# A convolution pair on one core: the residual added by the storing DMA, and TensorE's pieces dealt out anew

## The reference

```
x1  = x  + blur4x4(gn(x))                      # layer 0, gn: 32 groups
out = x1 + sum over 9 taps of wgt[tap] * shifted(gn(x1))   # layer 1
wgt = w2 . relu(group_norm(d4_1x1(gn(x1), w1))) + b2
```

## Time and profile before

| | |
|---|---|
| time, median of 3 runs | 5196.06 us (5190.89 to 5196.19) |
| the profiled execution's own time | 5190.41 us |
| its span | 5188.6 us |
| first stage | to about 1150 us |
| busy: PE, DVE, ACT, POOL | 4650.8, 4464.1, 2864.1, 3903.4 us |
| DMA | 679.71 MB, 131 GB/s on average |

### The profile page before, as it was taken

How to read it: one execution, slowest core, us unless ns; L and a number is a source line. 1 busy time by engine, 2 the same in 40 slices (tenths; PEclk the granted TensorE clock), 3 DMA queues, 4 the chain that set the end, 5 groups by cost and what they waited for, 6 DMA issues and landing times.

```text
span 5188.6 us, 117277 instructions
## 1 busy us (share of the span) xinstructions
PE 4650.8 (90%) x39036; PEld 1648.4 (32%) x39036; DVE 4464.1 (86%) x7761; ACT 2864.1 (55%) x4642; POOL 3903.4 (75%) x1952
## 2 busy tenths in 40 slices
PE   8999999978989898988989898989898989898965
PEld 3333333322333232333333232323232323232322
DVE  6777777734989898989899999989898989898998
ACT  7999999955444444444445454444444444444421
POOL 6888888833878787777777787778787868787888
PEclk9999999989999999999999999999999999999987
DMA  8999999943333233333333233333332323332321
GB/s 237 257 257 257 257 256 256 247 107 90 102 102 115 87 113 97 106 99 103 99 103 109 93 111 99 106 95 115 99 111 91 115 91 111 99 116 90 105 71 65
DMA packets 872972, 679.71 MB, mean 131 GB/s; under 512 B 560224, under 2 KB 822752, under 8 KB 856032
## 3 DMA queue, kind: packets, MB, share of 16 engines
q1 hardware_dynamic: 872416, 672.79, 44.2%
HBM read 404.21 MB, written 268.44 MB: 130 GB/s over the span
## 4 chain that ended last, share of the span: by engine, by line
PE 40%; DVE 16%; issue 12%; POOL 7%; ACT 3%; DVEq 0%; POOLq 0%; DMA 0%; SPq 0%; ACTq 0%
PE ps L801 8%; PE ps L748 7%; POOL acc L1054 7%; PE ps L803 6%; PE ps L738 6%; PE ps L789 5%; DVE prod_d L1105 5%; PE ps L776 5%; DVE prod_p L1105 4%; DVE ps L1149 3%; PE ps L763 2%; DVE ps L1105 2%; DVE six_t L1070 1%; DVE acc L1151 1%; ACT xh L901 1%
## 5 line engine op out<-in xcount | busy, mean ns | idle before, releaser
L1054 POOL TENSOR_TENSOR acc<-acc,prod_p 128x1024 f32<-128x1024 f32 x1280 | 3040.7, 2376 | 848.1 <-DVE acc L1151 701.0
L1105 DVE TENSOR_TENSOR prod_p<-ps,val 128x1024 f32<-128x1024 f32 x1280 | 1555.0, 1215 | 39.8 <-issue 27.8
L1105 DVE TENSOR_TENSOR prod_d<-ps,val 128x512 f32<-128x512 f32 x1536 | 1042.6, 680 | 10.7 <-ACT ps L959 10.7
L299 PE MATMUL ps<-xn,band 64*64 64x512 f32 x8192 | 948.0, 598 | 21.4 <-issue 12.9
L801 PE MATMUL ps<-acc,base 128*128 128x512 f32 x1024 | 620.6, 690 | 335.3 <-DVE prod_d L1105 311.2
L748 PE MATMUL ps<-xh,wh 128*32 128x512 f32 x6144 | 729.1, 602 | 70.5 <-ACT xm L909 24.8
L331 POOL TENSOR_TENSOR x_out<-x_out,x_in 128x512 f32<-128x512 f32 x512 | 636.4, 1275 | 0.0
L259 ACT ACTIVATE x_out<-ps 64x512 f32<-64x512 f32 x1024 | 606.2, 592 | 50.4 <-PE ps L299 28.7
L959 ACT ACTIVATE ps<-ps,b 128x256 f32<-128x256 f32 x576 | 236.7, 445 | 664.7 <-PE ps L789 661.4
L803 PE MATMUL ps<-prod_d,base 128*128 128x512 f32 x1024 | 589.4, 661 | 0.0
L776 PE MATMUL ps<-xm,base 128*32 128x256 f32 (+1 forms) x8192 | 574.8, 418 | 2.5 <-ACT xm L933 2.4
(11 more groups left out here) (76 smaller groups left out, 3706.8 us busy)
## 6 DMA issues: line engine op xcount, KB each, us to landing
x_in<-x SPq DMA_DIRECT2D x128, 1024.0 KB, 7.4
x<-x_out SPq DMA_DIRECT2D x256, 512.0 KB, 5.2
xr<-x SPq DMA_DIRECT2D x512, 256.0 KB, 3.4
acc<-x SPq DMA_DIRECT2D x1024, 128.0 KB, 3.1
out<-acc SPq DMA_DIRECT2D x256, 512.0 KB, 2.7
prod_p<-wsrc SPq DMA_DIRECT2D x1, 384.0 KB, 5.3
w<-w2t SPq DMA_DIRECT2D x1, 288.0 KB, 5.1
shift_m<-shifts SPq DMA_DIRECT2D x1, 256.0 KB, 5.7
```

Source lines behind the costliest of these rows:

```text
L299: mm = nc.tensor.matmul(ps[to:to + H2, 2 * two + t, :], band[rows, v, rows], group(xn[rows, k % N_RING, :], XP, W, v, 2 * two + x), start= ...
L1054: nc.gpsimd.tensor_tensor(acc[:, r, :], acc[:, r, :], prod_p[:, k % P_RING, :], ALU.add).then_inc(p_added, 1)
L1105: return nc.vector.tensor_tensor(dst.rearrange("p (m r w) -> p m r w", m=count, w=W), taps_of(tap).rearrange("p (m r w) -> p m r w", m=1, ...
```

## The change

The residual no longer goes through `acc` and TensorE. SyncE copies x1, in the output's layout, from DRAM to DRAM into `out` (two granules ahead as before); GpSimd, after the five adds of a granule, issues the storing DMA itself, with `accum_op=add`, so that the store adds `acc` onto the copy. For this GpSimd waits for its own last add and for the copy (`resid_in`). TensorE adds one product instead of two. VectorE waits for the store of four granules earlier before it writes `acc`. Values are made two granules ahead instead of three, the pieces stand in other half-steps, and the third block of statistics moves from granule 11 to 13.

```diff
-AHEAD = GRANS - 1
+AHEAD = GRANS - 2
-FORWARD_1 = {3: ((2, 1),), 5: ((3, 0),), 7: ((4, 1),), 9: ((5, 0),)}
-FORWARD_2 = {0: ((0, 0), (0, 1)), 1: ((1, 0), (1, 1)), 2: ((2, 0),), 5: ((3, 1),), 6: ((4, 0),), 9: ((5, 1),),
-             10: ((6, 0), (6, 1)), 12: ((7, 0), (7, 1))}
-BLOCK_V_1 = {1: ((0, 0), (0, 1)), 2: ((1, 0),), 6: ((3, 0), (3, 1)), 10: ((5, 0), (5, 1)), 14: ((7, 0), (7, 1))}
-BLOCK_V_2 = {2: ((1, 1),), 4: ((2, 0), (2, 1)), 8: ((4, 0), (4, 1)), 13: ((6, 0), (6, 1))}
-BLOCK_T_1 = {5: (2,), 9: (4,), 13: (7,)}
-BLOCK_T_2 = {1: (0,), 2: (1,), 6: (3,), 10: (5,), 12: (6,)}
-INVERSE_1 = {2: (0,), 3: (1,), 7: (3,), 11: (5,), 13: (6, 7)}
-INVERSE_2 = {5: (2,), 9: (4,)}
-LOAD_AT = {1: 1, 2: 2, 4: 3, 6: 4, 8: 5, 10: 6, 11: 7}
-LOAD_NEXT_AT = 13
+FORWARD_1 = {3: ((2, 1),), 5: ((3, 1),), 7: ((4, 1),), 10: ((6, 0), (6, 1)), 11: ((7, 0), (7, 1))}
+FORWARD_2 = {0: ((0, 0), (0, 1)), 1: ((1, 0), (1, 1)), 2: ((2, 0),), 4: ((3, 0),), 6: ((4, 0),),
+             8: ((5, 0), (5, 1))}
+BLOCK_V_1 = {1: ((0, 0),), 14: ((7, 0), (7, 1))}
+BLOCK_V_2 = {2: ((0, 1),), 4: ((1, 0), (1, 1)), 5: ((2, 0), (2, 1)), 6: ((3, 0), (3, 1)), 9: ((4, 0), (4, 1)),
+             10: ((5, 0), (5, 1)), 13: ((6, 0), (6, 1))}
+BLOCK_T_1 = {1: (0,), 2: (1,), 5: (2,), 6: (3,), 9: (5,), 12: (7,)}
+BLOCK_T_2 = {8: (4,), 10: (6,)}
+INVERSE_1 = {2: (0,), 7: (3,), 13: (7,)}
+INVERSE_2 = {2: (1,), 5: (2,), 9: (4,), 12: (5, 6)}
+LOAD_AT = {1: 1, 2: 2, 4: 3, 6: 4, 8: 5, 9: 6, 10: 7}
+LOAD_NEXT_AT = 12
...
-                dst = acc[32 * q:32 * q + 32, r, :].rearrange("p (m n) -> p m n", m=QM)
+                dst = out[img, at, 32 * q:32 * q + 32].rearrange("p (m n) -> p m n", m=QM)
                 sp.dma_start(dst, src).then_inc(resid_in[r], 16)
-        def store(i, n):                     # SyncE
-            wait_apart(sp, sp_apart, p_added, i * (NP * N_GRAN) + NP * (n + 1))
...
-            sp.dma_start(out[img, m], acc[:, n % ACC_RING, :]).then_inc(stored[n % ACC_RING], 16)
...
-            if half == 0:                    # add_two, now add_one
-                pe.wait_ge(resid_in[n % ACC_RING], i * (64 * N_GRAN // ACC_RING) + 64 * (n // ACC_RING + 1))
-            nc.tensor.matmul(ps[:, D_BANK, :], same, acc[:, n % ACC_RING, half * HALF:(half + 1) * HALF],
-                             start=False, stop=False, skip_group_check=True)
...
+        def store(i, n):                     # GpSimd, called after the five adds of granule n
+            r = n % ACC_RING
+            pool.wait_ge(p_added, i * (NP * N_GRAN) + NP * (n + 1))
+            pool.wait_ge(resid_in[r], i * (64 * N_GRAN // ACC_RING) + 64 * (n // ACC_RING + 1))
+            nc.gpsimd.dma_start(out[i, n], acc[:, r, :], accum_op=ALU.add).then_inc(stored[r], 16)
...
+            if a == 0 and not first(i, n - ACC_RING + 1):      # VectorE, before L1151
+                dve.wait_ge(stored[r], i * (16 * N_GRAN // ACC_RING) + 16 * (n // ACC_RING))
...
-            if more and n == 11:
+            if more and n == 13:
                 t_stats(i + 1, 2)
-            if more and n == 13:
                 t_stats(i + 1, 3)
```

More of the change, by code:

```diff
@@ L653, in load_x, with copy_resid @@
                 sp.dma_start(xr[:, kt, :].rearrange("p (q n) -> p q n", q=2), src).then_inc(x_loaded, 16)
-        def load_resid(i, n):
+        def copy_resid(i, n):
             u, q4, r = (n // GRANS) % UNITS, n % GRANS, n % ACC_RING
@@ L659, in load_resid @@
                 wait_apart(sp, sp_apart, stored[r], i * (16 * N_GRAN // ACC_RING) + 16 * (n // ACC_RING))
-            img = i + n // N_GRAN
+            img, at = i + n // N_GRAN, n % N_GRAN
             for q in range(BANDS):
@@ L663, in load_resid @@
                     :, q4 * QM:(q4 + 1) * QM, (q * 16 + u * UR) * W:(q * 16 + (u + 1) * UR) * W]
-                dst = acc[32 * q:32 * q + 32, r, :].rearrange("p (m n) -> p m n", m=QM)
+                dst = out[img, at, 32 * q:32 * q + 32].rearrange("p (m n) -> p m n", m=QM)
                 sp.dma_start(dst, src).then_inc(resid_in[r], 16)
-        def store(i, n):
-            wait_apart(sp, sp_apart, p_added, i * (NP * N_GRAN) + NP * (n + 1))
-            img, m = (i + n // N_GRAN, n % N_GRAN) if n >= 0 else (i - 1, n + N_GRAN)
-            sp.dma_start(out[img, m], acc[:, n % ACC_RING, :]).then_inc(stored[n % ACC_RING], 16)
         sp.dma_start(base[:], basis[:, 0:4 * P]).then_inc(base_in, 16)
@@ L681, in _, with period @@
             load_x(0, c)
-        load_resid(0, 0)
-        load_resid(0, 1)
+        copy_resid(0, 0)
+        copy_resid(0, 1)
         load_x(1, 0)
-        def period(i, more=True, ahead=True, begin=False):
+        def period(i, more=True, ahead=True):
             for n in range(N_GRAN):
@@ L692, in period @@
                 if more or n + 2 < N_GRAN:
[L693 to L697, removed]
+                    copy_resid(i, n + 2)
+        period(0)
         with sp.Fori(1, B - 2) as i:
@@ L701, in _ @@
         period(B - 1, more=False, ahead=False)
-        store(B - 1, N_GRAN - 1)
         for r in range(ACC_RING):
+            sp.wait_ge(resid_in[r], 64 * B * N_GRAN // ACC_RING)
             sp.wait_ge(stored[r], 16 * B * N_GRAN // ACC_RING)
@@ L794, in tap_weights, with add_one @@
                 mm.then_inc(tap_mm, 1)
-        def add_two(i, n, half):
+        def add_one(i, n, half):
             pe.wait_ge(own, i * (OWN * N_GRAN) + OWN * n + OWN // 2 * half + 2)
-            if half == 0:
-                pe.wait_ge(resid_in[n % ACC_RING], i * (64 * N_GRAN // ACC_RING) + 64 * (n // ACC_RING + 1))
-            nc.tensor.matmul(ps[:, D_BANK, :], same, acc[:, n % ACC_RING, half * HALF:(half + 1) * HALF],
-                             start=False, stop=False, skip_group_check=True)
             nc.tensor.matmul(ps[:, D_BANK, :], same, prod_d[:, 0, :], start=False, stop=True, skip_group_check=True)\
@@ L835, in _ @@
         values(1)
-        values(2)
         def half_step(i, n, of_t, of_inverse, of_v, of_forward):
@@ L851, in period @@
                 u = n // GRANS
-                add_two(i, n, 0)
+                add_one(i, n, 0)
                 if n % GRANS == 0 and not (begin and n == 0):
@@ L862, in period @@
                         values(1)
-                        values(2)
-                add_two(i, n, 1)
+                add_one(i, n, 1)
                 if more:
@@ L987, in _ @@
         keep_values(0, 1)
-        keep_values(0, 2)
         def keep_half_step(i, n, of_t, of_inverse, of_v, of_forward):
@@ L1015, in period @@
                         keep_values(i + 1, 1)
-                        keep_values(i + 1, 2)
                         relu(i + 1, 0)
@@ L1056, in period @@
                         t_rstd_of(i + 1)
+                store(i, n)
         period(0)
```

## The result

The changed kernel takes 5064.98 us (median of 4 runs, 5061.32 to 5067.52) against 5193.48 for the kernel before beside it (5189.98 to 5196.19): a ratio of 0.9752, 95% interval 0.9736 to 0.9769. The forecast was 5088. The profiled span is 5065.8 us, 122.8 shorter than before. In the new file L1142 is the old L1149, L1146 the old L1151, L1098 makes the products, L793 is TensorE's add, L1046 GpSimd's adds, L1035 its DMA, L666 the copies.

The account below looks back on a forecast made before the run. VectorE and TensorE, both near 91% busy, took turns as the bound. -16.4 + 3.5 + 4.6 + 1.2 = -7.1 us an image, -106 over 15, then -4 and +2: 5082 profiled, 5088 median; range 4990 to 5250.

Parts of the forecast that it names:

- TensorE off VectorE's path: Second stage: without the residual's matmul, VectorE's wait for TensorE falls from 16.4 to 3.5 us an image, gaining 12.9.
- GpSimd the new bound, by a little: GpSimd's adds plus a 1.2 us store take 13.65 us a granule against VectorE's 13.23: 4.6 us an image.
- The last image: Its granules, 13.9 us each before, would take 13.65 (-4 us); the last store, issued later, adds 2.
- my own formula: Change an image for an issue of d us: -16.4 + 3.5 + d + 11 (d - 0.78); gain gone at 1.79.
- The 13.23: Time in us that VectorE needs for a granule in which it does not wait.
- the ring: Four product buffers between VectorE and GpSimd: last pooled product begins 10.2 us after VectorE's last sum, needing four adds, 10.0.
- the slack can't be saved up: With only four product buffers, GpSimd's store costs 0.42 us in each of 11 granules without extra VectorE work.
- The image's change: Where images turn, the store of granule 13 stands between GpSimd's power and granule 14: cost 1.2 us.
- The hidden issue: Rival: GpSimd's store issue takes 0.78 us or less and VectorE is the bound: 5010 us; chance 0.17.
- Slower by the issue: Rival: GpSimd's issue makes it the bound in earnest: 5284 us at 2.2, 5382 at 2.7; chance 0.18.
- A product of VectorE in flight: Rival: GpSimd's issue waits for VectorE's running product, up to 1.2 us more, 2.4 in all: 5324 us; chance 0.04.
- Half clock: Rival: TensorE, less busy, is granted a mean clock of 0.8 and holds VectorE again: 5190 us; chance 0.11.

Follow-up runs that it names:

- tap1_twice: The changed kernel with tap 1's product added twice by TensorE, one matmul more in each half: 5187.84 us, ratio 0.9990 to the kernel before.
- dma_old_order: The changed kernel with the old order of TensorE's pieces, values three granules ahead and third statistics after granule 11: 5056.58 us, ratio 0.9736 to the kernel before.
- sync_plain: The changed kernel with SyncE storing acc plainly, the residual left out of the output and no DMA on GpSimd: 4960.70 us, ratio 0.9551 to the kernel before.
- store_behind: The changed kernel with GpSimd's store of granule n-1 issued after the fifth add of granule n: 5009.09 us, ratio 0.9644 to the kernel before.
- two_issues: The changed kernel with each GpSimd store split into two DMAs of 64 partitions, same bytes: 5212.36 us, ratio 1.0038 to the kernel before.

## Why the prediction was right, point by point

**TensorE off VectorE's path: right.** The wait fell from 16.4 us an image to 2.4; I left 3.5. tap1_twice shows that with the second add back the wait is back, 12.8 us an image. I dealt out the new order with care as if it were needed: dma_old_order shows that it isn't, at this pace. TensorE's busy time fell by 399 us, not by 500: the adds lost 576 (620.6 and 589.4 before, 633.5 after), but the mean block matmul went from 602 to 630 ns and the tap weights from 391 to 401, at a granted clock of 0.95 where it was 0.97 in the images of the earlier trace rows. These two make 66 of the 177 us between; the rest was not separated.

**GpSimd the new bound, by a little: right in kind, wrong in sizes that cancel.** The store takes 1.58 us in the loop, not 1.2. The DMA row is 0.88; the rest is the wait for the last add, 0.64 before a DMA that overlaps little of the next add. The last image, with a wait of 0.30, has the forecast's rhythm (13.66 from 4881.91 to 4895.57, against 13.65). By my own formula 1.58 would have given -12.9 + 1.58 + 11 x 0.80 = -2.5 us an image, -38, with +2 in the last image and +2 at its end: 5162 as a median. Two things stood on the other side.

First, VectorE's pace. The 13.23 was one granule. From VectorE's second sum in a granule to that of the next, as a mean over the 14 images of the loop, the shortest granules of the kernel before already take 13.36 to 13.39 us, and those of sync_plain 13.37. I had written that the ring gives 10.0 us to four adds against 10.2, and took that 0.2 for slack; it was none.

Second, the number of granules that pay. By the same means only seven of the 16 (granules 3, 4, 5, 8, 11, 12 and 13) take about 14.04 us, 0.67 more than in sync_plain. Granules 1, 2, 6, 7, 9 and 10 take what they take there: 13.4, or 15.5 with statistics, or 14.5 in granule 1. I had written that the slack can't be saved up. But beside statistics GpSimd waits for VectorE (0.81 at 2757.34), and the granule after that is again at 13.4; that the first is the cause of the second is my reading. The image's change (granules 14, 15 and 0) costs 2.0 and not 1.2. So the store costs 7 x 0.67 + 2.0 = 6.7 us an image against sync_plain (240.8 and 234.1), and the forecast was 4.6 + 1.2 = 5.8. A longer store, a slower VectorE and fewer granules that pay came out near that by luck.

**The sum.** By the waits, -14.0 and +5.7 make -8.2 an image; the images lost 8.2 (122.4 over 15), and I had -7.1. That the waits agree so well is luck too: all of VectorE's that the view lists fell by 136 us, 14 more than the images lost, so 14 us went elsewhere, into gaps or instructions that it does not list. The last image: -3.5 for -4; its end: +4.8 for +2, of which 2.9 is the landing (5.6 us after the issue for an accumulating store, 2.7 for the plain one in the earlier trace rows).

**What cost nothing, as said.** Neither VectorE nor GpSimd waits for `stored` or `resid_in`. SyncE itself does wait for the stores ahead of its copies, and nobody waits for SyncE. L946's wait for a product is gone from ScalarE and dma_old_order, whose values are three ahead still, lost nothing by it.

**The rivals.** The hidden issue (5010) did not come, but store_behind is close to that case: in line only 0.87 us, 5009, though by other terms (granules of 13.38 and not 13.23). Slower by the issue: two_issues, with 2.4 us in line, has nearly its slope (180 us for each us against some 196), and comes out at 5212 where I had 5324 for 2.4; the gain would end at 2.3 us and not at 1.79, for the reasons above. A product of VectorE in flight: the 256 issues take 877 to 1064 ns, 880 in the median, beside a VectorE that is 95% busy. What the Trainium skill, SBUF — State Buffer, Who interferes with whom, says of two-port modes does not show with `tensor_tensor` here, as the page has it. Half clock: the images kept 0.95. The estimate by the Trainium skill, DMA: Bandwidth & Descriptors, Specifications, was 5052; the measured time is 13 us above it, and the page's figure to the first byte is not what GpSimd's queue paid: 0.88 us, and 1.58 with the wait.

## What to carry to other kernels

An instruction put in line on an engine with little slack costs what it takes and the wait it brings along; its place decides. Follow every ring between two engines round once and count what stands in it: moving the store behind the next granule's first add was worth nothing, behind its fifth 56 us. When an engine ceases to be the bound, an order made for it may be worth nothing until the next bound is mended.

## What was not expected of the hardware

The same instruction pair, last add and DMA that waits for it, shows an idle of 0.64 us in the rolled loop and 0.30 in the last image; the loop's DMA has two register instructions of 37 and 29 ns ahead of it (224 of the 256), which are too short to be all of the difference. It was not separated further. The DMA row overlaps the add behind it: the add seems to begin 0.61 us after the DMA's start, and its five take 12.78 instead of 12.45. An issue of a DRAM-to-DRAM copy takes SyncE 0.574 us where the load into `acc` took some 0.32.
